# Where three weights are asked for at the start of a graph kernel, and one product of the constant fewer

## The chip, the core and the metric

The kernel runs on one core of a Trainium2 chip. Five engines work side by side, each through its own list of instructions, and wait for each other by semaphores: TensorE (PE; its weight loads are shown apart, as PEld), VectorE (DVE), ScalarE (ACT), GpSimd (POOL) and SyncE (SP). SyncE and ScalarE ask for DMA transfers, each on a queue of its own. The metric is the device time of one execution in microseconds (us); less is better.

## The reference

Sixty-four graphs of 128 nodes with 256 features go through two layers, each with a residual sum and a normalisation over the features:

```python
# layer 0: x, adj -> ReLU of the sum of three hops
Xw = X @ Wv + bv
sj = Xw @ aw[:d, 0]; si = Xw @ aw[d:, 0]
e = leaky_relu(sj[:, None, :] + si[:, :, None] + ab[0], negative_slope=0.2)
alpha = A * exp(e)
transition = alpha / (sum(alpha, axis=-1, keepdims=True) + 1e-12)
for k in range(3):
    H = H + Xk @ Wk[k] + bk[k]
    Xk = transition @ Xk
x = layernorm(x + relu(H))
# layer 1
x = layernorm(x + (adj @ x) @ w)
```

## The kernel before, in words

The graphs are worked on in 32 pairs. Each engine has one hand-written list: a start, a loop `step(k)` over the pairs, and an end. The lists are staggered; in step k of TensorE the products of W2 for pair k + 5, of W1 (and W0) for pair k + 1, the attention sums of pairs k and k + 1 and the second layer of pairs k - 1 and k - 2 are in flight.

A float32 product is made of three products of halves: ScalarE rounds a tile to its `_hi` part, GpSimd or VectorE subtracts to get the `_lo` part, and TensorE multiplies hi with hi, hi with lo, and lo with hi (line 1073). The first pair's products with W2 and W1 are taken from the full float32 tiles (`first_product`, line 1101), so that they need no split.

The start, which the change touches:

- SyncE asks for xt(0) (line 314), the transposed Wv (`WvT_sb`, line 356) and W1 (line 352), waits for xt(0), and asks for W0 (line 352) and xt(1). It waits for W2, asks for adjs(0), waits for W1, asks for xt(2) and xt(3), waits for xt(1), and asks for adjs(1), w, adjs(2) and nodes(0). Then `step(-5)` begins; from its fourth xt on, SyncE also waits for TensorE (`v1_done`) and GpSimd (`xt_lo_ready`).
- ScalarE asks for W2 (`WY_sb`, line 404), the small vectors (`vectors_sb`, 3 KB, line 405), bk (line 406) and ab (line 407). Then it loads its table and rounds: `xt_hi(0)`, `wx_hi(0)` (needs W0), `v2_hi(0)` (needs the first products of W2), `xt_hi(1)`, `first_scores()`, `xt_hi(2)`, `leaky_of(0)`, `exponentials(0)`, and so on.
- TensorE multiplies a constant by itself nine times (`keep_warm`, line 1236; 128x128 by 128x512 in bf16, with no use for the result). Then come `first_hop2(0)` (xt(0) and W2, first graph), `score_weights()` (Wv transposed times the attention vectors, line 1269; needs `WvT_sb` and `vectors_sb`), `first_hop2(1)`, `first_hop1(0)` (xt(0) and W1, needs W1 and VectorE's copy of the score weights), `score_shift()`, `first_hop1(1)`, `sum_of_biases()`, `spread_scores(0)` (needs ScalarE's first scores), `hop0(0)` and `hop2_and_scores(1)` (12 matmuls each), and `propagate_v2(0)`, the first to need alpha.
- VectorE copies the score weights beside W1 and W2 and splits W2. GpSimd sums the bias vectors (needs `vectors_sb`) and then makes `xt_lo(0)`.

W0, W1, W2, Wv, w and each xt and nodes are 256 KB; each adjs is 128 KB.

Of the kernel before, what the change touches and what calls it, by code (L numbers as in the profile page):

```python
# [10 lines left out]
P = 128  # L11
PER = 2
DMA = 16
# [5 lines left out]
def resnorm_graph_kernel(nc, xt, adjs, nodes, WvT, vectors, ab, Wk, bk, w, si_rows, out):  # L19
# [6 lines left out]
    with ExitStack() as ctx:  # L26
        def sb(name, shape, dt=F32):
            return ctx.enter_context(nc.sbuf_tensor(name, shape, dt))

        def ps(name, shape):  # L30
            return ctx.enter_context(nc.psum_tensor(name, shape, F32))

        def sem(name):
            return ctx.enter_context(nc.semaphore(name))
# [11 lines left out]
        WvT_sb = sb("WvT_sb", [P, C, D])  # L46
# [68 lines left out]
        ps_v = ps("ps_v", [P, PER, 512])  # L115
# [11 lines left out]
        xt_loaded = [sem(f"xt_loaded{s}") for s in range(4)]  # L127
# [3 lines left out]
        WvT_loaded = sem("WvT_loaded")  # L131
# [115 lines left out]
        def there(k):  # L247
            return 0 <= k < PAIRS
# [57 lines left out]
        @block.sync  # L306
        def _(sp):
            def load_xt(k):
                if k == 4:

                    sp.wait_ge(v1_done, 1)
                if k >= 4:
                    sp.wait_ge(xt_lo_ready, k - 3)
                sp.dma_start(xt_sb[k % 4][:], xt[k]).then_inc(xt_loaded[k % 4], DMA)

            def load_adjs(k):
                if k >= 5:

                    sp.wait_ge(agg_done, k - 4)
                sp.dma_start(adjs_sb[k % 5][:].rearrange("p b i -> p (b i)"),  # L320
                             adjs[k]).then_inc(adjs_loaded[k % 5], DMA)

            def load_nodes(k):
                if k >= 2:
                    sp.wait_ge(res1_ready, k - 1)
                sp.dma_start(nodes_sb[k % 2][:].rearrange("p b d -> p (b d)"),
                             nodes[k]).then_inc(nodes_loaded[k % 2], DMA)

            def store(k):
                if k < LAST - 4:  # L330
                    sp.wait_ge(out_ready, k + 1)
                else:
                    sp.wait_ge(late_out_ready, k - (LAST - 4) + 1)
                sp.dma_start(out[k],
                             out_sb[k % 3][:].rearrange("p b d -> p (b d)")).then_inc(stored[k % 3], DMA)

            def store_si(k):
                sp.wait_ge(scores_ready, k + 1)
                sp.dma_start(si_rows[k], scores[k % 3][:, 1]).then_inc(si_stored, DMA)  # L339

            def load_spread(k):

                sp.wait_ge(si_stored, DMA * (k - BY_PE + 1))
                if k >= 3:
                    sp.wait_ge(leaky_ready, k - 2)
                sp.dma_start(spread[k % 3][:].rearrange("p j b -> p (j b)"),
                             si_rows[k].rearrange("j b -> (j b)").partition_broadcast(P)
                             ).then_inc(spread_loaded[k % 3], DMA)

            def load_Wk(n):  # L350
                to = (W0_sb, W1_sb)[n]
                sp.dma_start(to[:, :, 0:D], Wk[n].rearrange("(c p) n -> p c n", p=P)).then_inc(Wk_loaded[n], DMA)


            load_xt(0)
            sp.dma_start(WvT_sb[:], WvT.rearrange("(c p) n -> p c n", p=P)).then_inc(WvT_loaded, DMA)
            load_Wk(1)
            sp.wait_ge(xt_loaded[0], DMA)
            load_Wk(0)
            load_xt(1)  # L360
            sp.wait_ge(Wk_loaded[2], DMA)
            load_adjs(0)
            sp.wait_ge(Wk_loaded[1], DMA)
            load_xt(2)
            load_xt(3)
            sp.wait_ge(xt_loaded[1], DMA)
            load_adjs(1)
            sp.dma_start(w_sb[:], w.rearrange("(c p) n -> p c n", p=P)).then_inc(w_loaded, DMA)
            load_adjs(2)
            load_nodes(0)  # L370

            def step(k):
                if there(k + 3) and k + 3 >= BY_PE:
                    load_spread(k + 3)
                if there(k + 4) and k + 4 >= BY_PE:
                    store_si(k + 4)
                if k == -3:
                    load_adjs(3)
                    load_nodes(1)
                if there(k + 1) and k > 0:  # L380
                    load_nodes(k + 1)
                if there(k + 3) and k > 0:
                    load_adjs(k + 3)
                if there(k + 9) and k >= -5:
                    load_xt(k + 9)
                if there(k - 3):
                    store(k - 3)

            for k in range(-5, LAST + 2):
                step(k)  # L390

            sp.wait_ge(late_half_out_ready, 1)
            sp.dma_start(out[LAST - 1, :, 0:D], out_sb[(LAST - 1) % 3][:, 0]).then_inc(last_stored, DMA)
            for b in range(PER):
                sp.wait_ge(last_out_ready, b + 1)
                sp.dma_start(out[LAST, :, b * D:(b + 1) * D], last_out_sb[:, b]).then_inc(last_stored, DMA)
            for slot in range(3):
                sp.wait_ge(stored[slot], DMA * len(range(slot, LAST - 1, 3)))

            sp.wait_ge(last_stored, 2 * PER * DMA)  # L400

        @block.scalar
        def _(act):
            act.dma_start(WY_sb[:, :, 0:D], Wk[2].rearrange("(c p) n -> p c n", p=P)).then_inc(Wk_loaded[2], DMA)
            act.dma_start(vectors_sb[:].rearrange("p c n -> p (c n)"), vectors).then_inc(vectors_loaded, DMA)
            act.dma_start(bk_sb[:], bk).then_inc(bk_loaded, DMA)
            act.dma_start(ab_col[:], ab.partition_broadcast(P)).then_inc(ab_loaded, DMA)

# [660 lines left out]
        def _(pe):  # L1069
# [35 lines left out]
            def first_hop2(b):  # L1105
                pe.wait_ge(xt_loaded[0], DMA)
                pe.wait_ge(Wk_loaded[2], DMA)
                last = first_product(ps_y[:, b, 0:D], WY_sb[:, :, 0:D], b)
                if b == PER - 1:
                    last.then_inc(y_done, 1)  # L1110
# [122 lines left out]
            def keep_warm(to, times):  # L1233

                for n in range(times):
                    pe.matmul(to, some[:, 0:P], some, start=True, stop=True, skip_group_check=True)  # L1236
# [77 lines left out]
                    aggregate(k - 1)  # L1314
                hop2_and_scores(k + 5, [1] if k == 1 else range(PER))

            keep_warm(ps_v[:, 0], 9)
            first_hop2(0)
            score_weights()
            first_hop2(1)  # L1320
# [68 lines left out]
```

## Time and profile before

| | before |
|---|---|
| median of 3 runs | 275.74 us |
| lowest and highest | 275.46 and 275.97 us |
| span of the profiled execution, first to last instruction | 273.8 us |
| busy: TensorE products / weight loads | 98% / 90% |
| busy: VectorE / ScalarE / GpSimd | 80% / 69% / 71% |

Busy shares are averages over the whole span. "Idle before, releaser" in a row tells how long an engine stood idle and what ended it; where a wait is for several things, the one named is the last that the profile shows, and it need not be the one that held. Products of TensorE are pipelined and their ends are modelled, so the distance from start to start is the better measure. The time of a DMA to landing counts from the start of its issue.

### The profile page before, as it was taken

What the parts mean: (1) busy time and instruction counts of PE and PEld (TensorE: products, weight loads), DVE (VectorE), ACT (ScalarE), POOL (GpSimd) and SP (SyncE); (2) the same over time, 40 slices, a digit from 0 to 9 for tenths busy, and PEclk for the clock granted to TensorE, in tenths of its full rate; (3) what the DMA queues carried; (4) which work ended last, traced back from release to release, by engine and by line L of the source; (5) the groups of instructions that cost most, each with busy time, mean ns of one, the idle gap of its engine ahead of it and who ended that gap; (6) DMA issues with size and microseconds to landing.
All of it is one profiled execution on the core that took longest, in us unless ns stands there. A gap on an engine that the chain in (4) does not pass through costs nothing.

```text
span 273.8 us, 6042 instructions
## 1 busy us (share of the span) xinstructions
PE 267.3 (98%) x1899; PEld 247.7 (90%) x1899; DVE 218.1 (80%) x615; ACT 187.9 (69%) x428; POOL 194.6 (71%) x419
## 2 busy tenths in 40 slices
PE   8999998999999999999999999999999999999993
PEld 4899988999999999999999999999999999999992
DVE  0777668888898888889888888988888898788895
ACT  2788666776667777666777766677776667765653
POOL 2576537878777787877777787777778777557564
PEclk9999999999999999999999999999999999999998
DMA  7848256458593388555873456843884348822204
GB/s 224 292 141 94 44 185 97 94 150 154 149 149 123 91 123 141 162 143 153 94 117 122 145 157 141 144 110 108 120 159 98 116 115 111 118 66 77 95 25 153
DMA packets 28758, 34.91 MB, mean 127 GB/s; under 512 B 7091, under 2 KB 16694, under 8 KB 28726
## 3 DMA queue, kind: packets, MB, share of 16 engines
q1 hardware_dynamic: 28016, 34.12, 56.4%
q10 hardware_dynamic: 710, 0.40, 0.5%
q8 instruction: 15, 0.25, 0.4%
q14 instruction: 17, 0.14, 0.2%
HBM read 26.09 MB, written 8.42 MB: 126 GB/s over the span
## 4 chain that ended last, share of the span: by engine, by line
PE 86%; DMA 5%; DVE 3%; ACT 2%; issue 1%; SPq 1%; POOL 1%; POOLq 0%; DVEq 0%; ACTq 0%
PE ps_v L1073 27%; PE ps_y L1073 14%; PE ps_out L1073 14%; PE ps_h L1073 10%; PE ps_agg L1246 9%; DMA si_rows_dram<-scores 3%; PE ps_v L1183 2%; PE ps_v L1187 2%; PE ps_v L1185 2%; DMA nodes<-nodes_dram 2%; PE ps_v L1236 1%; PE ps_y L1101 1%; SPq L339 1%; PE ps_v L1101 1%; DVE stats L777 1%
## 5 line engine op out<-in xcount | busy, mean ns | idle before, releaser
L1073 PE MATMUL ps_v<-WX_hi,XT_hi 128*128 128x512 f32 (+1 forms) x128 | 47.7, 373 | 0.0
L1073 PE MATMUL ps_v<-WX_lo,XT_hi 128*128 128x512 f32 (+1 forms) x128 | 47.4, 371 | 0.0
L1073 PE MATMUL ps_v<-WX_hi,XT_lo 128*128 128x512 f32 (+1 forms) x128 | 47.4, 370 | 0.0
L986 POOL TENSOR_TENSOR alpha<-exps,adjs 128x256 f32<-128x256 f32 x31 | 23.1, 746 | 31.3 <-ACT exps L462 26.0
L974 POOL TENSOR_TENSOR XT_lo<-xt,XT_hi 128x512 fp32r<-128x512 f32 x32 | 41.3, 1291 | 4.8 <-DVE WX_lo L891 2.7
L990 POOL TENSOR_TENSOR alpha_lo<-alpha,alpha_hi 128x256 fp32r<-128x256 f32 x31 | 22.9, 737 | 18.4 <-ACT alpha_hi L471 18.4
L494 ACT ACTIVATE y<-res,offset,rstd 128x256 f32<-128x256 f32 x62 | 33.6, 591 | 1.1 <-POOL offset L945 1.1
L1073 PE MATMUL ps_y<-WY_hi,XT_hi 128*128 128x258 f32 x112 | 34.1, 305 | 0.0
L1246 PEld LDWEIGHTS ps_agg<-adjs,y 128*128 128x128 f32 x248 | 32.0, 191 | 2.2
L1246 PE MATMUL ps_agg<-adjs,y 128*128 128x128 f32 x248 | 32.6, 274 | 0.0
L487 ACT ACTIVATE V_hi<-ps_v 128x512 fp32r<-128x512 f32 x32 | 19.1, 596 | 19.5 <-PE ps_v L1073 19.3
L1073 PE MATMUL ps_out<-w_hi,agg_hi 128*128 128x256 f32 x112 | 31.6, 282 | 0.0
L1073 PE MATMUL ps_y<-WY_hi,XT_lo 128*128 128x258 f32 x112 | 31.6, 282 | 0.0
L1073 PE MATMUL ps_y<-WY_lo,XT_hi 128*128 128x258 f32 x112 | 31.5, 282 | 0.0
L1073 PE MATMUL ps_out<-w_hi,agg_lo 128*128 128x256 f32 x112 | 31.3, 280 | 0.0
L1073 PE MATMUL ps_out<-w_lo,agg_hi 128*128 128x256 f32 x112 | 31.3, 279 | 0.0
L968 POOL TENSOR_SCALAR out_sb<-res,rstd,offset 128x256 f32<-128x256 f32 x54 | 29.6, 559 | 0.1
L479 ACT ACTIVATE ps_v<-ps_v,inv_rowsum 128x256 f32<-128x256 f32 x62 | 25.2, 444 | 5.5 <-DVE inv_rowsum L677 3.1
L1073 PEld LDWEIGHTS ps_v<-WX_hi,XT_lo 128*128 128x128 f32 x128 | 24.0, 188 | 4.6
L500 ACT ACTIVATE agg_hi<-ps_agg 128x512 fp32r<-128x512 f32 x31 | 18.5, 598 | 13.2 <-PE ps_agg L1246 13.2
L1073 PEld LDWEIGHTS ps_v<-WX_hi,XT_hi 128*128 128x128 f32 x128 | 24.1, 188 | 3.8 <-ACT ps_v L479 0.3
L1073 PEld LDWEIGHTS ps_v<-WX_lo,XT_hi 128*128 128x128 f32 x128 | 24.1, 188 | 3.4
(168 smaller groups left out, 831.5 us busy)
## 6 DMA issues: line engine op xcount, KB each, us to landing
xt<-xt_dram SPq DMA_DIRECT2D x32, 256.0 KB, 5.6
nodes<-nodes_dram SPq DMA_DIRECT2D x32, 256.0 KB, 5.6
out_dram<-out_sb SPq DMA_DIRECT2D x30, 256.0 KB, 5.3
adjs<-adjs_dram SPq DMA_DIRECT2D x32, 128.0 KB, 5.6
spread<-si_rows_dram SPq DMA_DIRECT2D x29, 128.0 KB, 4.9
W_sb<-Wk_dram SPq DMA_DIRECT2D x2, 256.0 KB, 3.8
si_rows_dram<-scores SPq DMA_DIRECT2D x29, 1.0 KB, 3.7
WY_sb<-Wk_dram ACTq DMA_DIRECT2D x1, 256.0 KB, 4.0
```

The costliest lines, as they stand in the source:

```text
L479: act.activation(ps_v[:, b, 0:D], ps_v[:, b, 0:D], ACT.Copy, scale=inv_rowsum[k % 2][:, b:b + 1]).then_inc(v_scaled, 1)
L487: act.activation(V1_hi[:], ps_v[:, :, 0:D], ACT.Copy).then_inc(v1_hi_ready, 1)
L494: last = act.activation(y[k % 3][:, b], res1[:, b], ACT.Identity, bias=offset1[:, b:b + 1], scale=rstd1[:, b:b + 1])
L500: act.activation(agg_hi[k % 2][:], agg(k), ACT.Copy).then_inc(agg_hi_ready, 1)
L968: last = pool.tensor_scalar(out_sb[k % 3][:, b], res2[k % 2][:, b], rstd2[k % 3][:, b:b + 1], offset2[k % 3][:, b:b + 1], ALU.mult, ALU.add)
L974: pool.tensor_tensor(XT_lo[k % 7][:].rearrange("p c b i -> p (c b i)"), xt_sb[k % 4][:], XT_hi[k % 7][:].rearrange("p c b i -> p (c b i)") ...
L986: pool.tensor_tensor(alpha[:], exps[:], adjs_sb[k % 5][:], ALU.mult).then_inc(alpha_ready, 1)
L990: pool.tensor_tensor(alpha_lo[k % 2][:], alpha[:], alpha_hi[k % 2][:].bitcast(F32), ALU.subtract).then_inc(alpha_lo_ready, 1)
L1073: last = pe.matmul(to, a, b, start=start and n == 0, stop=stop and n == 2, skip_group_check=True)
L1101: last = pe.matmul(to, X[:, c, b], weights[:, c], start=c == 0, stop=c == C - 1, skip_group_check=True)
L1183: pe.matmul(ps_v[:, b, 0:D + 2], alpha_hi[k % 2][:, b], V2_hi[k % 4][:, b], start=True, stop=False, skip_group_check=True)
L1246: last = pe.matmul(agg(k)[:, c, b], y[k % 3][:, b, c * P:(c + 1) * P], adjs_sb[k % 5][:, b], start=True, stop=True, skip_group_check=True)
```

## The change

Wv is asked for by ScalarE, after W2 and the small vectors, instead of by SyncE. SyncE asks for W1 after its wait for xt(0), and no longer ahead of it. TensorE makes eight products of the constant instead of nine. The amount of data and all later instructions are the same.

```diff
             load_xt(0)
-            sp.dma_start(WvT_sb[:], WvT.rearrange("(c p) n -> p c n", p=P)).then_inc(WvT_loaded, DMA)
+            sp.wait_ge(xt_loaded[0], DMA)
             load_Wk(1)
-            sp.wait_ge(xt_loaded[0], DMA)
             load_Wk(0)
             load_xt(1)
             sp.wait_ge(Wk_loaded[2], DMA)
@@
             act.dma_start(WY_sb[:, :, 0:D], Wk[2].rearrange("(c p) n -> p c n", p=P)).then_inc(Wk_loaded[2], DMA)
             act.dma_start(vectors_sb[:].rearrange("p c n -> p (c n)"), vectors).then_inc(vectors_loaded, DMA)
+            act.dma_start(WvT_sb[:], WvT.rearrange("(c p) n -> p c n", p=P)).then_inc(WvT_loaded, DMA)
             act.dma_start(bk_sb[:], bk).then_inc(bk_loaded, DMA)
             act.dma_start(ab_col[:], ab.partition_broadcast(P)).then_inc(ab_loaded, DMA)
@@
-            keep_warm(ps_v[:, 0], 9)
+            keep_warm(ps_v[:, 0], 8)
```

## Rows read from the trace of the kernel before

**Rows 1.** Busy us (and count) by engine, granted clock, DMA share, by stretch.

```profile
core 0: us, PE busy (x) PEld busy (x) DVE busy (x) ACT busy (x) POOL busy (x), PEclk, DMA share, GB/s
40.00:42.00 2.00, 0.88 (x8) 0.67 (x7) 1.93 (x7) 1.04 (x4) 1.84 (x7) 1.00 0.60 207
...
45.00:85.00 40.00, 40.00 (x283) 37.22 (x282) 33.38 (x96) 28.76 (x67) 31.31 (x66) 1.00 0.67 133
```

**Rows 2.** Waits of the weight loads, whole span: total us, times, longest us.

```profile
PEld ps_h L1073 <- DVE V_lo L709: 1.5, 2, 1.3
```

**Rows 3.** The tile nodes, the one transfer issued between 30 and 32 us.

```profile
DMA to landing us min/median/max: 7.2/7.2/7.2
```

**Rows 4.** Timeline of TensorE's products: start us, us (first start to last end).

```profile
0.76 4.00 PE L1236 MATMUL ps_v<-const-bfloat16-1.0 128*128 128x512 bf16 x9 [0.76 <-PEq L1380]
...
4.12 0.63 PE L1236 MATMUL ps_v<-const-bfloat16-1.0 128*128 128x512 bf16 x1
...
4.86 1.42 PE L1101 MATMUL ps_y<-WY_sb,xt 128*128 128x256 f32 x4
...
5.68 0.60 PE L1101 MATMUL ps_y<-WY_sb,xt 128*128 128x256 f32 x2
```

**Rows 5.** Timeline of SyncE's queue, the issues of the first 4.9 us.

```profile
0.72 0.38 SPq L314 DMA_DIRECT2D xt<-xt_dram  x1
1.16 0.42 SPq L356 DMA_DIRECT2D WvT_sb<-WvT_dram  x1
1.63 2.77 SPq L352 DMA_DIRECT2D W_sb<-Wk_dram  x2
```

**Rows 6.** The tile xt: xt(0) and xt(1) (one row), then xt(2), issued at 6.30.

```profile
DMA to landing us min/median/max: 3.3/3.3/3.3
...
DMA to landing us min/median/max: 3.4/3.4/3.4
```

**Rows 7.** Timeline of ScalarE and its queue, first 4.9 us.

```profile
0.73 0.47 ACTq L404 DMA_DIRECT2D WY_sb<-Wk_dram  x1
...
1.75 0.56 ACTq L406 DMA_DIRECT2D bk_sb<-bk_dram  x1
...
2.72 1.28 ACT L412 ACT_TABLE_LOAD   x1 [2.72 <-issue]
```

**Rows 8.** DMA issues: KB each, median us from issue to landing.

```profile
nodes<-nodes_dram SPq DMA_DIRECT2D x32, 256.0 KB, 5.6
...
WY_sb<-Wk_dram ACTq DMA_DIRECT2D x1, 256.0 KB, 4.0
WvT_sb<-WvT_dram SPq DMA_DIRECT2D x1, 256.0 KB, 4.3
...
vectors_sb<-vectors_dram ACTq DMA_DIRECT2D x1, 3.0 KB, 4.4
```

**Rows 9.** DMA queues from 0 to 3.5 us: packets, MB, share of 16 engines.

```profile
q10 hardware_dynamic: 116, 0.12, 9.5%
```

**Rows 10.** The same from 3.5 to 4.2 us.

```profile
q10 hardware_dynamic: 153, 0.14, 57.9%
q1 hardware_dynamic: 123, 0.13, 50.5%
```

**Rows 11.** The same from 4.2 to 5 us.

```profile
q10 hardware_dynamic: 146, 0.01, 11.7%
```

**Rows 12.** Timeline of all engines from 5.9 to 10.3 us.

```profile
5.90 1.08 PEld L1269 LDWEIGHTS ps_out<-vectors_sb,WvT_sb 128*128 128x128 f32 x8
...
7.08 0.63 ACT L417 ACTIVATE WX_hi<-W_sb 128x512 fp32r<-128x512 f32 x1 [2.41 <-DMA W_sb<-Wk_dram]
...
7.66 0.84 PEld L1101 LDWEIGHTS ps_v<-W_sb,xt 128*128 128x128 f32 x4
...
8.07 0.60 ACT L442 ACTIVATE V_hi<-ps_y 128x512 fp32r<-128x512 f32 x1 [0.36 <-PE ps_y L1101]
...
10.04 0.26 ACT L428 ACTIVATE scores<-ps_v,shift 128x4 f32<-128x4 f32 x1 [0.85 <-PE ps_v L1101]
10.20 0.62 ACT L412 ACTIVATE XT_hi<-xt 128x512 fp32r<-128x512 f32 x1
```

## The prediction

> **What bounds the kernel now.** I read the table by stage first. From 45 us on TensorE has work in all of its time, 40.00 us of 40.00; before that it has gaps, the largest between 40 and 42 us [rows 1]. So nothing that the change touches can make the long middle shorter. It touches only the loading at the start, and a gain there counts as far as it moves everything behind it forward. The waits of the weight loads name one long wait after the start, 1.3 us for a V_lo of VectorE [rows 2]. That V_lo stands in VectorE's order behind the residual of pair 2, which needs nodes(2), and nodes(2) took 7.2 us to land [rows 3]. I return to it as a rival.
>
> Then the start itself. Nine products of the constant run from 0.76, the last from 4.12: (4.12 - 0.76) / 8 = 0.42 us for 512 columns, which is 1.2 GHz. The last one's columns are through at about 4.54, and the first product of X starts at 4.86, not at 4.54 [rows 4]. The view names xt as the releaser, but xt(0) was asked for at 0.72 and took 3.3 us, so it was there at 4.02 [rows 5, 6]. W2 was asked for at 0.73 and took 4.0 us: 4.73 [rows 7, 8]. So W2 ends TensorE's wait, and the last 0.2 to 0.3 us before 4.86 are a wait for a DMA that one product of the constant fewer does not shorten. The clock is still low there: the first two half products of X take 5.68 - 4.86 = 0.82 us, while the two from 5.68 on lie 0.60 - 0.38 = 0.22 us apart. The clock rose to 2.4 GHz at about 5.5 [rows 4]. (The granted-clock column shows 1.00 for this stretch too, so I read the level from the spacing.)
>
> **Part 1: what stands beside W2 in the DMA engines.** Up to 3.5 us the ScalarE queue (q10) moved 0.12 MB, from there to 4.2 another 0.14 MB; together that is W2's 0.26 MB, so its data was through at about 4.2. In the second stretch SyncE's queue (q1) moved 0.13 MB, nearly all of it Wv [rows 9, 10]. In the new kernel q1 has nothing behind xt(0) until W1 is asked for at about 4.0. W2's last 0.14 MB then have the engines alone: at the rate of that stretch, 0.27 MB in 0.70 us or 386 GB/s, 0.36 us instead of 0.70. W2 lands some 0.33 us earlier, at 4.40. The bounds: 0 (the bandwidth was not what held it) and 0.71 (W2 as early as xt(0), 4.02; W0 needed 3.05 us from issue, 4.03, to its use at 7.08, with others beside it [rows 5, 12]). I take 0.33, because both queues show their bytes in just that stretch.
>
> **Part 2: one product of the constant fewer.** It ends at 4.12 instead of 4.54. With W2 at 4.40, plus the 0.13 us from landing to start (4.86 - 4.73), the first product of X starts at 4.53. With nine products it would have started at about 4.54 too. So this edit by itself is worth nothing, to 0.1 us: it only takes away a bound that would just begin to hold. If W2 lands at once with xt(0), it is worth up to 4.54 - 4.15 = 0.39 us of start, half of that in time.
>
> What does the earlier start give? Until about 5.5 the clock is low. Work begun 0.33 us earlier runs those 0.33 us at half speed, so from 5.5 on TensorE is 0.33 / 2 = 0.16 us ahead. The ends are 0 and 0.71 / 2 = 0.35 us.
>
> **Part 3: Wv on ScalarE's queue.** Before, it landed at 1.16 + 4.3 = 5.46 [rows 5, 8], and the weights of its products were loaded from 5.90 on, behind the products of X and without a wait [rows 12]. In the new kernel they could start at 5.74. Wv is asked for after the small vectors, at 1.75, when bk was before [rows 7]. In the engines it follows W2 (through at 3.87) and the vectors. Its own 0.26 MB at 386 GB/s take 0.67 us, and from data to landing W2 took 4.73 - 4.2 = 0.53. That makes 3.87 + 0.67 + 0.53 = 5.07 if the vectors' 128 rows cost nothing. They took most of the 0.8 us from 4.2 to 5.0 (146 packets, 0.01 MB) beside a full q1 [rows 11]: 5.87 at that price. I take the middle, 5.5: no wait. A wait at the upper end is 5.87 - 5.74 = 0.13 us. The other upper bound is the vectors' own 4.4 us from issue [rows 8]: 1.75 + 4.4 = 6.15, and with Wv's data behind that 6.82. It is the slower rival.
>
> ScalarE's own instructions shift by one issue, some 0.5 us: bk and ab are asked for later, the table load runs 3.2 to 4.5 instead of 2.72 to 4.00 [rows 7], and XT_hi(0) behind it ends by 5.2. The next activation starts at 7.08 after 2.41 us of idling [rows 12], and GpSimd takes XT_hi(0) up only behind its work on the vectors, which land at 1.2 + 4.4 = 5.6 [rows 7, 8]. So this is hidden, by 0.4 us of cover at the least.
>
> **Part 4: W1 behind xt(0) on SyncE's queue.** SyncE stands on xt(0) until 4.03 (1.63 + 2.77, less the 0.37 of W0's own issue). Before, W0 was asked for then and was in use 3.05 us later, at 7.08 [rows 5, 12]. Now W1 takes that place: 7.08 at the latest, where it had been there at 6.30, when SyncE went on to xt(2). TensorE wants it after the second half of W2's products, at 7.66 - 0.16 = 7.50 [rows 12]: 0.42 us of cover. W0 is one issue later (0.42 us, Wv's): about 7.5. It holds ScalarE's WX_hi, which started at 7.08, until 7.5; it then ends at 8.13, and V_hi follows, which started at 8.07 after 0.36 us of idling [rows 12]. That cover is all but used up; what is over, some 0.1 us, goes into the 0.85 us that ScalarE idles before the first scores. xt(1) lands at 4.9 + 3.3 = 8.2 [rows 6], before that V_hi is done. Behind the wait for W1 stand xt(2) and xt(3): asked for at 7.08 instead of 6.30, xt(2) lands at 7.08 + 3.4 = 10.5 [rows 6] where its XT_hi started at 10.20 [rows 12], and the first attention scores stand behind that on ScalarE. This could cost 0.3 us of ScalarE's time, and 0.46 against the shifted order; but what waits on it, the first alpha, is wanted by TensorE only behind 12 matmuls with W0 and 12 with W2. I take 0, with 0.3 as the upper bound; W1 landing sooner than W0 did, with less ahead of it in q1, speaks for 0.
>
> **Sum.** Span 273.8 - 0.16 = 273.6 us. The median of the runs before lies 1.94 us above the span of the profiled one (275.74 against 273.8), and that stays: 275.74 - 0.16 = 275.6 us.
>
> **The rivals.**
> *Nothing moves (0.20).* W2 was late for its own latency. TensorE then starts at 4.86 again, with 0.74 us of empty array ahead instead of 0.32. For it: xt(0) had the engines with half of W2 only and still took 3.3 us. Against it: the bytes of Wv that went in between [rows 10]. Time: 275.7. The Trainium skill points this way: DMA: Bandwidth & Descriptors, "Issuing engines are not separate DMA queues", says that DMAs from any engine share the same 16 DMA engines and interleave, so that another issuer saves only issue time. By that rule alone moving Wv would bring nothing. But the change also keeps W1 back, and between 3.5 and 4.2 us the two queues did share the engines [rows 10]; so I give the rule's result the smaller chance.
>
> *Wv comes late: slower (0.13).* Wv stands behind three rows of work on ScalarE's queue. It costs from the point where it lands after 5.64 (its products at 5.74). At 6.15 the net is 0.51 - 0.16 = +0.35: 276.1; at 6.82 it is 1.18 - 0.16 = +1.02: 276.8. All that follows waits: u, both W1 products, the scores. Over 0.55 us of loss needs a landing after 6.35.
>
> *A gap in the constant's products delays the clock: slower (0.05).* Low clock lasted from 0.76 to 5.5. Each microsecond more of it costs half a microsecond. Against it: at 40 to 42 us TensorE idled 1.1 us and the clock stayed up [rows 1], though that is a clock already up. One more microsecond: 275.74 + 0.5 - 0.16 = 276.1.
>
> *The late stall moves: faster (0.12).* nodes(2) took 7.2 us where the median of all 32 is 5.6 [rows 3, 8]. Had it taken 5.6, VectorE would go on 1.6 us earlier, and the 1.3 us in which TensorE waits [rows 2] would be gone. A shifted order of DMAs could do this: 275.6 - 1.3 = 274.3. Against it: the runs before agree to 0.5 us, and nothing in the change reaches that transfer but 0.16 us of shift.
>
> *Forecast (0.50):* 275.6, of itself 275.2 to 275.9.
>
> **Range and chances.** The measurement can tell 0.2% from no change, 0.55 us. The forecast and "nothing moves" lie inside; even the upper end of the start's gain, 0.35 us, does. Faster by more: the late stall, and a little for a gain of 0.35 with the scatter of the runs: 0.16. Slower by more: the far half of the late Wv, the clock, and a missed cover in part 4: 0.14. Same: 0.70. The range 274.9 to 276.2 leaves out the moved stall and the far end of the late Wv.
>
> **What would show it.** Right: the first product of X at 4.5 to 4.6, W2 landing in 3.6 to 3.8 us; the products of Wv directly behind, without a wait; W0 in ScalarE's WX_hi at about 7.5; the first scores on ScalarE at about 9.9 instead of 10.04; everything from 14 us on 0.1 to 0.2 us earlier. Wrong: the first product of X again at 4.86; a wait of the weight loads of Wv's products or of the W1 products on a DMA; low-clock spacing after 5.6; another length of the wait at 41 us, which would outweigh all else.

## The result, and the profile after

| | before | changed |
|---|---|---|
| median | 275.27 us | 276.4 us |
| lowest and highest, 22 executions each | 274.3 and 276.4 us | 274.79 and 280.91 us |
| ratio, with its 95% interval | | 1.0044 (1.0026 to 1.0061) |
| span of the profiled execution | 273.8 us | 273.1 us |

The change is slower, by over 0.2%. The median is 276.4, above the upper end of the range (276.2). Seven of the 22 executions took over 277.5 us, and none of before did. The ratios, here and below, leave out executions more than 1.5% above the fastest of their kernel, here the two longest of these seven (279.61 and 280.91 us), so they understate the loss.

The profiled execution of the changed kernel was one of its quick ones, 274.87 us. It shows what the moved transfers do, and not what makes the median. Its page, busy time and share of the span:

```profile
span 273.1 us, 6040 instructions
...
PE 266.9 (98%) x1898; PEld 247.6 (91%) x1898; DVE 217.9 (80%) x615; ACT 188.0 (69%) x428; POOL 194.0 (71%) x419
```

The start in the view in order of time (start, length, engine, line, operation, idle before and releaser), to be read against [rows 4 to 7, 12]. First TensorE and its weight loads:

```profile
0.76 3.57 PE L1236 MATMUL ps_v<-const-bfloat16-1.0 128*128 128x512 bf16 x8 [0.76 <-PEq L1380]
4.77 1.50 PE L1101 MATMUL ps_y<-WY_sb,xt 128*128 128x256 f32 x4 [0.45 <-DMA WY_sb<-Wk_dram]
...
5.89 1.08 PEld L1269 LDWEIGHTS ps_out<-vectors_sb,WvT_sb 128*128 128x128 f32 x8
6.11 0.95 PE L1269 MATMUL ps_out<-vectors_sb,WvT_sb 128*128 128x2 f32 x8
6.92 1.11 PE L1101 MATMUL ps_y<-WY_sb,xt 128*128 128x256 f32 x4
...
8.88 1.12 PE L1101 MATMUL ps_v<-W_sb,xt 128*128 128x258 f32 x4
...
10.55 0.43 PE L1165 MATMUL ps_out<-identity,scores 128*128 128x128 f32 x2
```

Then the queues of ScalarE and SyncE, and ScalarE's work:

```profile
1.74 0.46 ACTq L405 DMA_DIRECT2D WvT_sb<-WvT_dram  x1
...
3.96 0.90 SPq L352 DMA_DIRECT2D W_sb<-Wk_dram  x2
4.90 0.47 SPq L314 DMA_DIRECT2D xt<-xt_dram  x1
...
6.71 0.80 SPq L314 DMA_DIRECT2D xt<-xt_dram  x2
...
7.42 0.63 ACT L417 ACTIVATE WX_hi<-W_sb 128x512 fp32r<-128x512 f32 x1 [2.27 <-DMA W_sb<-Wk_dram]
...
8.98 0.63 ACT L412 ACTIVATE XT_hi<-xt 128x512 fp32r<-128x512 f32 x1 [0.31 <-DMA xt<-xt_dram]
...
10.03 0.26 ACT L428 ACTIVATE scores<-ps_v,shift 128x4 f32<-128x4 f32 x1 [0.43 <-PE ps_v L1101]
...
10.49 0.63 ACT L412 ACTIVATE XT_hi<-xt 128x512 fp32r<-128x512 f32 x1 [0.20 <-DMA xt<-xt_dram]
```

The first product of X starts at 4.77, where it had started at 4.86 [rows 4]. The products of Wv follow at 6.11, without a wait for a DMA, as before, and the last product of W1 (8.88) and the step behind the scores (10.55) stand where they stood, to 0.01 us. ScalarE's WX_hi begins 0.34 us later than it did [rows 12] and its XT_hi(2) 0.29 us later, while the first scores stand where they stood. ScalarE now waits 0.31 us for xt(1) ahead of XT_hi(1), whose start in the trace of before was 8.57.

The DMA issues, with the median time to landing in the last column, against [rows 8]; and ScalarE's queue (packets, MB, share of 16 engines) up to 3.5 us, against [rows 9]:

```profile
WY_sb<-Wk_dram ACTq DMA_DIRECT2D x1, 256.0 KB, 3.9
...
WvT_sb<-WvT_dram ACTq DMA_DIRECT2D x1, 256.0 KB, 3.6
```

```profile
q10 hardware_dynamic: 246, 0.19, 16.0%
```

ScalarE's queue had 0.19 MB through by 3.5 us, against 0.12 [rows 9]. Yet W2 landed at 0.72 + 3.9 = 4.62 (4.64, if the 0.13 us from landing to start are as before), and not 0.33 us earlier. Neither difference is steady: two more traces of this same kernel (e7 and e14 below) have 0.14 and 0.03 MB through by 3.5 us, and their first product of X starts at 4.82 and 5.09. Around 41 us, against [rows 1, 2]:

```profile
PEld ps_h L1073 <- DVE V_lo L709: 0.6, 2, 0.5
```

The wait for V_lo is 0.5 us at the longest, where it had been 1.3. That, 0.8 us, is as much as the two spans differ by (0.7 us); the experiments below show that it scatters from trace to trace.

### The profile page after: what moved, and what is told of

It reads as the page before. It is cut to its first block, busy times and chain, and to the rows that moved or that the text cites. A ratio compares the mean times of both kernels' runs of the same rounds, so it can differ in the third digit from the quotient of the medians.

```text
span 273.1 us, 6040 instructions
## 1 busy us (share of the span) xinstructions
PE 266.9 (98%) x1898; PEld 247.6 (91%) x1898; DVE 217.9 (80%) x615; ACT 188.0 (69%) x428; POOL 194.0 (71%) x419
## 4 chain that ended last, share of the span: by engine, by line
PE 86%; DMA 6%; DVE 2%; SPq 1%; POOL 1%; ACT 1%; issue 1%; POOLq 0%; DVEq 0%; ACTq 0%
PE ps_v L1073 27%; PE ps_y L1073 14%; PE ps_out L1073 14%; PE ps_h L1073 10%; PE ps_agg L1246 9%; DMA si_rows_dram<-scores 3%; PE ps_v L1183 3%; PE ps_v L1187 3%; PE ps_v L1185 3%; DMA nodes<-nodes_dram 2%; DMA WY_sb<-Wk_dram 1%; PE ps_y L1101 1%; SPq L339 1%; PE ps_v L1101 1%; DVE stats L777 1%
```

## The experiments

Each ran in five rounds beside the kernel before. The edits are against the kernel before unless another is named. The expectations call the theories by letters. C: with the array empty ahead of the first product of X, the clock rises late. V: Wv comes late. X: xt(2), asked for behind the wait for W1, comes late. P: xt(1) comes late, and GpSimd's subtraction then runs beside VectorE's first alpha. L: the wait at 41 us makes the difference, through nodes(2) and adjs(4). D: the two DMA edits by themselves cost 0.55 us. "Long" is an execution above 277.5 us.

### The edits one by one

```diff
-            keep_warm(ps_v[:, 0], 9)
+            keep_warm(ps_v[:, 0], 8)
```

> Only edit: eight products of the constant instead of nine; every DMA as before. Theory X (a late xt(2) costs the time; it comes of W1 being held back): 1.000 within 0.002, the first product of X at 4.8 to 4.9 as before. Theory C (the emptier TensorE ahead of the first product of X makes the clock rise late in some executions, half a us per us): 1.003 or more, with single runs several us long. Theory V (Wv lands late in some executions): 1.000.

Measured: 276.18 us (274.48 to 279.31) against 275.32, ratio 1.0011 (0.998 to 1.0042), 5 long of 12. Its profiled execution is a long one, span 277.5:

```profile
0.76 3.57 PE L1236 MATMUL ps_v<-const-bfloat16-1.0 128*128 128x512 bf16 x8 [0.76 <-PEq L1380]
4.96 2.05 PE L1101 MATMUL ps_y<-WY_sb,xt 128*128 128x256 f32 x4 [0.63 <-DMA WY_sb<-Wk_dram]
6.80 1.71 PE L1269 MATMUL ps_out<-vectors_sb,WvT_sb 128*128 128x2 f32 x8
8.36 2.05 PE L1101 MATMUL ps_y<-WY_sb,xt 128*128 128x256 f32 x4
10.21 1.93 PE L1101 MATMUL ps_v<-W_sb,xt 128*128 128x258 f32 x4
```

The four products of W2 take 2.05 us each time, where the same four take 1.11 us at the high clock (6.92 in the changed kernel), and the eight of Wv 1.71 us, not 0.95. This is 1.2 GHz, until about 13.5 us. One product of the constant fewer, alone, brings the long executions.

```diff
-            sp.dma_start(WvT_sb[:], WvT.rearrange("(c p) n -> p c n", p=P)).then_inc(WvT_loaded, DMA)
@@
+            act.dma_start(WvT_sb[:], WvT.rearrange("(c p) n -> p c n", p=P)).then_inc(WvT_loaded, DMA)
```

> Only edit: Wv asked for on ScalarE's queue behind W2 and the small vectors; W1 stays ahead of SyncE's wait for xt(0), nine products of the constant. Theory X: 1.000 within 0.002 (W1 and xt(2) as early as before or earlier). Theory C: 1.000. Theory V: 1.003 or more, and the products of Wv waiting on a DMA after 5.9.

Measured: 276.46 (274.6 to 277.84), ratio 1.0027 (0.9997 to 1.0058).

```profile
5.03 1.33 PE L1101 MATMUL ps_y<-WY_sb,xt 128*128 128x256 f32 x4 [0.27 <-DMA WY_sb<-Wk_dram]
6.63 1.02 PE L1269 MATMUL ps_out<-vectors_sb,WvT_sb 128*128 128x2 f32 x8 [0.27 <-DMA WvT_sb<-WvT_dram]
```

Here the products of Wv do wait for Wv, 0.27 us, and start 0.51 us later than before (6.12); part of that is the later start of X (5.03). Wv took 4.8 us to land, against 3.5 to 4.1 in the nine traces that also hold W1 back. So the rival was real as long as W1 was asked for early; with W1 held back, it is not. Three executions lie at 277.54 to 277.84, with a lower recorded clock (0.989 to 0.990); none was profiled, and what they are stays open.

```diff
-            load_Wk(1)
             sp.wait_ge(xt_loaded[0], DMA)
+            load_Wk(1)
```

> Only edit: W1 asked for after SyncE's wait for xt(0); Wv stays on SyncE, nine products of the constant. Theory X: 1.003 to 1.005, xt(2) asked for some 0.4 us later than 6.30, XT_hi(2) at about 10.5 instead of 10.20 and propagate_v2(0) at about 13.97 instead of 13.81. Theories C and V: 1.000.

Measured: 275.76 (275.14 to 276.19), ratio 1.001 (0.9985 to 1.0035), none long. No difference that can be told.

Both edits of the transfers, with nine products (e2's and e3's together):

> Both DMA edits together, nine products of the constant. Theory X: 1.004, as the whole change. Theory C: 1.000, because the ninth product fills the wait for W2 as before. Theory V: 1.004.

Measured: 275.8 (275.1 to 276.55), ratio 1.0021 (1.0003 to 1.0039), none long.

```profile
9.78 0.63 ACT L412 ACTIVATE XT_hi<-xt 128x512 fp32r<-128x512 f32 x1 [0.93 <-DMA xt<-xt_dram]
...
10.48 2.54 POOL L974 TENSOR_TENSOR XT_lo<-xt,XT_hi 128x512 fp32r<-128x512 f32 x2 [3.42 <-ACT XT_hi L412]
...
12.35 0.95 DVE L635 TENSOR_TENSOR alpha<-exps,adjs 128x256 f32<-128x256 f32 x1 [0.86 <-ACT exps L462]
```

```profile
14.49 0.36 PE L1183 MATMUL ps_v<-V_hi,alpha_hi 128*128 128x258 f32 x1 [0.57 <-DVE alpha_lo L639]
```

xt(1) took 4.7 us to land, so ScalarE waited 0.93 us for it. GpSimd's two subtractions ran until 10.48 + 2.54 = 13.02, beside VectorE's first alpha. That took 0.95 us, and TensorE's first product with alpha started at 14.49. The same two lines in the trace of before:

```profile
12.20 0.42 DVE L635 TENSOR_TENSOR alpha<-exps,adjs 128x256 f32<-128x256 f32 x1 [0.51 <-ACT exps L462]
...
13.81 0.36 PE L1183 MATMUL ps_v<-V_hi,alpha_hi 128*128 128x258 f32 x1
```

### How many products of the constant

```diff
-            keep_warm(ps_v[:, 0], 9)
+            keep_warm(ps_v[:, 0], 7)
```

> Only edit against the kernel before: seven products of the constant. TensorE is then empty from 3.7 to the first product of X at 4.9. Theory C (emptier TensorE ahead of the first product of X makes the clock rise late in some executions): more such executions than with eight (five of 12 there above 277.5 us): half or more above 277.5, ratio 1.006 to 1.012. Rival (the count of products is of no account, the long runs with eight were of the chip): none above 277.5, ratio 1.000.

Measured: 278.52 (275.54 to 279.22), ratio 1.0113 (1.0073 to 1.0152), 5 long of 6.

```profile
4.87 2.05 PE L1101 MATMUL ps_y<-WY_sb,xt 128*128 128x256 f32 x4 [0.97 <-DMA WY_sb<-Wk_dram]
```

The same with 10 in place of 7:

> Only edit against the kernel before: ten products of the constant, the last one's columns through at about 4.97. Theory C: no execution above 277 us, ratio 0.998 to 1.001 (the first product of X up to 0.15 us later at the low clock, no late rise). Rival: 1.000 with the same scatter as before.

Measured: 275.61 (274.35 to 276.68), ratio 1.0003 (0.998 to 1.0025), none long. With 7, 8, 9 and 10 products ahead of X in the kernel before, 5 of 6, 5 of 12, 2 of 165 (the runs of before of all sessions) and 0 of 12 executions are long.

The changed kernel once more, with no edit:

> The changed kernel once more, word for word, for more executions of it and another profile. Theory C: a quarter to a half of the executions above 277.5 us, where the two kernels with W1 held back and nine products had none of 24; ratio 1.004 to 1.008. If the profile falls on a long one, the low-clock spacing of 0.42 us lasts far beyond 6 us.

Measured: 277.04 (274.94 to 279.69), ratio 1.0037 (1.0008 to 1.0067), 6 long of 12.

The changed kernel with 10 products:

```diff
-            keep_warm(ps_v[:, 0], 8)
+            keep_warm(ps_v[:, 0], 10)
```

> The change, but with ten products of the constant instead of eight. Theory C: no execution above 277.5 us (the change itself had 13 of 34), and what is left is the cost of the DMA edits, 1.001 to 1.003. Rival (the long executions are made by the DMA edits together with fewer products): still some above 277.5.

Measured: 275.65 (274.42 to 276.47) against 275.39, ratio 1.0005 (0.9991 to 1.0019), none long. Two products more in the changed kernel take away its long executions and nearly all of its loss. What the tenth product costs at the start cannot be read from single traces. The last product of W1, at 8.88 before and in the change, stands 0.34 and 0.62 us later in e6's and e9's:

```profile
9.22 1.12 PE L1101 MATMUL ps_v<-W_sb,xt 128*128 128x258 f32 x4
```

```profile
9.50 1.12 PE L1101 MATMUL ps_v<-W_sb,xt 128*128 128x258 f32 x4
```

But in e13's trace, also with ten, it stands at 8.62, and in six with nine (e3, e4, e8, e11, e12, e16) at 8.39 to 9.16. What moves it is mostly the rise of the clock, which the traces' own clock records put at 6.13 us in e6, 6.70 in e9 and 4.78 in e13. The ratios of e6 and e9, 1.0003 and 1.0005, show no cost either.

Eight products, and the ninth behind the first two of X's groups (the kernel before; the amount of work is the same):

```diff
-            keep_warm(ps_v[:, 0], 9)
+            keep_warm(ps_v[:, 0], 8)
             first_hop2(0)
+            keep_warm(ps_v[:, 0], 1)
```

> The kernel before, but the ninth product of the constant stands behind the first two products of X and W2 instead of ahead of them: the amount of work in the first 6 us is the same, the emptiness ahead of the first product of X is that of eight. Theory C (it is the emptiness ahead of that product that counts): a third or more of the executions above 277.5 us, ratio 1.002 to 1.008. Rival (the total of products counts): none above 277.5, ratio 1.000 to 1.001.

Measured: 275.93 (274.91 to 280.12), ratio 1.0018 (0.9992 to 1.0045), 5 long of 12. So the place counts, ahead of the first product of X, and not the number. No run separates the two things that the missing product changes there: the unbroken work is shorter by one product, and the gap behind it is longer.

```profile
4.94 1.10 PE L1101 MATMUL ps_y<-WY_sb,xt 128*128 128x256 f32 x4 [0.61 <-DMA WY_sb<-Wk_dram]
5.88 0.38 PE L1236 MATMUL ps_v<-const-bfloat16-1.0 128*128 128x512 bf16 x1
```

This trace is of a quick execution: it waits as long ahead of X as e1's (4.94 and 4.96), and the clock was high at once (its record has the rise at 4.44, within the gap). So the length of the wait alone does not decide a single execution. What does stays open.

The changed kernel a third time, with no edit:

> The changed kernel word for word, a third time. Theory C: a quarter to a half of the executions above 277.5 us; a profile of one of them shows the products of X at the low-clock spacing (0.42 us from start to start instead of 0.22) to beyond 9 us and everything behind 3 to 4 us later. Rival (with the change the long executions have another cause than the one traced with eight products alone): a profiled long execution with its clock risen at about 5.5.

Measured: 277.22 (274.73 to 279.85) against 275.32, ratio 1.0055 (1.0021 to 1.0088), 6 long of 12; the mean of all twelve is 277.24. This time the profiled execution is a long one, 278.45 us with a span of 276.6:

```profile
0.76 3.57 PE L1236 MATMUL ps_v<-const-bfloat16-1.0 128*128 128x512 bf16 x8 [0.76 <-PEq L1380]
5.09 2.05 PE L1101 MATMUL ps_y<-WY_sb,xt 128*128 128x256 f32 x4 [0.76 <-DMA WY_sb<-Wk_dram]
6.93 1.71 PE L1269 MATMUL ps_out<-vectors_sb,WvT_sb 128*128 128x2 f32 x8
8.50 2.05 PE L1101 MATMUL ps_y<-WY_sb,xt 128*128 128x256 f32 x4
10.35 1.93 PE L1101 MATMUL ps_v<-W_sb,xt 128*128 128x258 f32 x4
12.06 0.42 PE L1276 MATMUL ps_agg<-const-float32-1.0,bv_aw_sum 128*128 128x1 f32 x2
12.35 1.12 PE L1101 MATMUL ps_v<-W_sb,xt 128*128 128x258 f32 x4
...
14.03 0.43 PE L1165 MATMUL ps_out<-identity,scores 128*128 128x128 f32 x2
```

Against the quick execution of the same kernel, above: everything up to 12.06 runs at half speed, and from 12.35 on the lengths are those of the quick one. The step behind the scores starts at 14.03, where the quick one has it at 10.55: 3.48 us, and the spans differ by 276.6 - 273.1 = 3.5. What is lost at the start is never given back, since TensorE has no idle time from 45 us on to give it from [rows 1]. The traces' clock records agree: the rise is at 12.36 us here and at 5.58 in the quick execution, 6.8 us more at half speed, 3.4 us.

### What the moved transfers cost

e4, with xt(2) no longer held back by W1:

```diff
             load_adjs(0)
-            sp.wait_ge(Wk_loaded[1], DMA)
             load_xt(2)
```

> Both DMA edits, nine products, and SyncE no longer waits for W1 before it asks for xt(2) and xt(3) (they go into other buffers, so nothing else changes). Theory X (the DMA edits cost because xt(2), adjs(1) and what follows come late): xt(2) asked for at about 6.1 instead of 6.97, XT_hi(2) without a wait at 10.3, the weight loads of propagate_v2(0) without their 0.7 us wait; ratio 1.000, against 1.002 with the wait. Rival (the loss of the DMA edits is elsewhere, or scatter): 1.002 again.

Measured: 276.09 (274.9 to 278.19), ratio 1.0035 (1.0014 to 1.0056).

```profile
9.62 0.63 ACT L411 ACTIVATE XT_hi<-xt 128x512 fp32r<-128x512 f32 x1 [0.69 <-DMA xt<-xt_dram]
```

xt(2) asked for earlier took nothing off the loss: theory X fell. The line shows xt(1), not xt(2), to be late. One execution is long (278.19, recorded clock 0.993; the two of before have 0.992 and 0.993).

The same trace shows an empty array that did no harm:

```profile
0.76 3.50 PE L1235 MATMUL ps_v<-const-bfloat16-1.0 128*128 128x512 bf16 x9 [0.76 <-PEq L1379]
5.19 1.10 PE L1100 MATMUL ps_y<-WY_sb,xt 128*128 128x256 f32 x4 [0.94 <-DMA WY_sb<-Wk_dram]
```

The nine products took 3.50 us and not 4.00, since the clock rose during them (at 3.61 by its record). TensorE then idled 0.94 us, longer than in e14's long execution (0.76), and the clock stayed up. In all four long executions that were profiled the gap lies ahead of the rise; a gap behind it, as here, did nothing.

e4, with xt(1) asked for ahead of W1 and W0:

```diff
             sp.wait_ge(xt_loaded[0], DMA)
+            load_xt(1)
             load_Wk(1)
             load_Wk(0)
-            load_xt(1)
```

> Both DMA edits, nine products, and SyncE asks for xt(1) ahead of W1 and W0 after its wait for xt(0). Theory P (the DMA edits cost because xt(1) lands up to 2 us later, GpSimd's XT_lo(1) and XT_lo(2) then run beside VectorE's first alpha, which takes 0.95 us instead of 0.42, and propagate_v2(0) starts at 14.49 instead of 13.81): XT_hi(1) without a wait for a DMA, alpha back at 0.42, propagate_v2(0) at 13.7 to 13.9, ratio 1.000 unless W1, now later, holds TensorE before its products at 7.7. Rival (the loss is elsewhere): 1.002 again.

Measured: 276.25 (275.19 to 276.61) against 275.39, ratio 1.0026 (1.0008 to 1.0044). XT_hi(1) still started at 9.51, now behind a WX_hi that waited for W0 until 8.50 (7.42 in the change), and XT_hi(2), at 10.97, waited 0.62 us. The wait went from one transfer to the next; this order on the queue does not cure it.

### The wait at 41 us

nodes(2) and adjs(4) are asked for in step 0 instead of step 1:

```diff
-                if there(k + 1) and k > 0:
+                if k == 0:
+                    load_nodes(2)
+                    load_adjs(4)
+                if there(k + 1) and k > 1:
                     load_nodes(k + 1)
-                if there(k + 3) and k > 0:
+                if there(k + 3) and k > 1:
                     load_adjs(k + 3)
```

> The kernel before, but SyncE asks for nodes(2) and adjs(4) in its step 0, behind the store of scores(4), instead of in step 1, behind the issue that takes 2.2 us at 28.3. Theory L (TensorE's 1.3 us wait at 41 us comes of nodes(2) and adjs(4) landing at 38, and its size, 0.3 to 1.7 us from trace to trace, is most of the scatter of the undisturbed runs): the residual of pair 2 and alpha(4) without a wait for a DMA, TensorE's wait at 41 us under 0.3, ratio 0.995 to 0.997. Rival (something else is late at 41 us): ratio 0.999 to 1.001.

Measured: 274.12 (273.72 to 274.71) against 275.32, ratio 0.996 (0.9942 to 0.9978).

```profile
PEld ps_h L1076 <- DVE V_lo L712: 0.2, 1, 0.2
```

```profile
23.53 0.43 SPq L326 DMA_DIRECT2D nodes<-nodes_dram  x1
...
28.36 2.60 SPq L339 DMA_DIRECT2D si_rows_dram<-scores  x1
```

SyncE's write of the scores at 28.3 us took 2.60 us to issue (2.27 in the trace of before, 2.18 in that of the change; the ordinary issue beside it 0.43). In the kernel before, nodes(2) stood behind it. Asked for ahead of it, it lands in time, the wait at 41 us is 0.2 us, and the twelve executions lie within 1.0 us, where those of before spread over 2.6 (273.63 to 276.27). By trace, that wait was 1.3 us before, 0.5 in the change, and 0.3 to 1.7 in the eleven traces of e1 to e11: it differs between executions of kernels that have the same work there.

The changed kernel with 10 products and this edit:

> Both DMA edits of the change, ten products of the constant, and nodes(2) and adjs(4) asked for in step 0. Theories C and L together: no execution above 277.5 us, ratio 0.996 to 0.999, some 0.001 to 0.002 above the same without the DMA edits. If the DMA edits' loss is only a shift of when the wait at 41 us is paid: the same ratio as without them.

Measured: 274.67 (274.27 to 274.96), ratio 0.9981 (0.9962 to 1.0001), none long. Against e12, of the same session, that is 0.55 us more.

e12 with 8 products:

> nodes(2) and adjs(4) early as before, Wv and W1 where the kernel before has them, eight products of the constant instead of nine. Theory C: two heaps of executions, one at 274.0 to 274.8 us as with nine products, the other (a quarter to a half of them) 3.2 to 4.2 us above. Rival (one product fewer costs nothing): one heap at 274.0 to 274.8.

Measured: 274.03 against 274.02, ratio 1.0021 (0.9989 to 1.0052). With the scatter gone, the two kinds of execution stand apart: nine at 273.75 to 274.38, and three at 277.75, 277.80 and 278.09. Nothing lies in the 3.37 us between. The profiled one is long:

```profile
4.86 2.04 PE L1104 MATMUL ps_y<-WY_sb,xt 128*128 128x256 f32 x4 [0.53 <-DMA WY_sb<-Wk_dram]
...
12.12 1.50 PE L1104 MATMUL ps_v<-W_sb,xt 128*128 128x258 f32 x4
```

e12 with both edits of the transfers and nine products:

> nodes(2) and adjs(4) early, both DMA edits, nine products of the constant. Theory D (the 0.55 us that the same kernel with ten products lies above the one without the DMA edits are the DMA edits): median 274.5 to 274.8. Rival (they are the tenth product): 274.1 to 274.3.

Measured: 274.43 (273.9 to 274.69) against 274.02, ratio 1.0009 (0.9999 to 1.0019), none long. So the transfers cost 0.4 us by the medians (the ratio's interval reaches from 0 to 0.5). The median lies between what theory D and its rival said, so how the 0.55 us are shared between the transfers and the tenth product stays open.

In this last session the kernel before took 274.02 us in the middle, without any edit (273.61 to 274.93), and in e16's trace the issue at 28 us was an ordinary one (the next, at 34.39, took 1.61 us); in e15's none was slow. So e12 beats both kernels by 0.4% in a session where the slow issue comes. That it gains nothing where the issue does not come is likely but not shown: neither e12 nor a trace of before was taken in the last session, only e15, whose nine quick executions lie where before's do.

## Why the prediction was wrong

**What bounds the kernel: right.** A loss at the start goes through to the end in full, 3.48 us of 3.5.

**Part 1, W2's landing: the 0.33 us did not come.** In the change's trace the landing moved from 4.73 to some 4.64, 0.09 us, and that is within the scatter: W2 took 3.8 to 4.3 us to land in the nine traces with both edits of the transfers (4.04 in the mean), and 4.0 to 4.3 in the seven with the transfers of before (4.09). Whether bandwidth beside W2 held it at all stays open; its share is far below 0.33 us. "Nothing moves" was right here. The Trainium skill points this way (DMA: Bandwidth & Descriptors, "Issuing engines are not separate DMA queues"): by that rule another issuer saves only issue time. The traces agree, with 4.04 against 4.09 us.

**Part 2, one product fewer: the step that decided.** It said that this edit is worth nothing, since it only takes away a bound that would just begin to hold. With W2 hardly earlier, it took away cover instead. The eighth product's columns are through at 0.76 + 8 × 0.42 = 4.12, and the array stood empty until 4.77 to 5.09 in the traces of the kernels with eight, 0.65 to 0.97 us, where before it was 0.32 (with nine products at the low clock, 0.60 at the most, in e12). In those kernels with the change's order (22 + 12 + 12 executions) 19 of 46 were long; in e1, e10 and e15 13 of 36. Of the kernels with nine or ten ahead of X, e3, e4, e6, e9, e11, e12, e13 and e16 had none in 95; before had 2 in 165, e8 1 in 12 and e2 3 in 12. These six lie at 277.54 to 278.19 with a recorded mean clock of 0.989 to 0.993, and none was profiled. They are probably of another kind, for the four long executions that were profiled have 0.997 to 1.000, as the quick ones have. Two of the long ones with eight products have 0.992 as well (280.91 in the change, 277.96 in e10), so the counts 19 and 13 may each be one too high. In the three long traces above, and in e5's, the clock stays at 1.2 GHz until 12 to 13.5 us.

**The clock rival: the right name, priced at a seventh and given 0.05.** It took one microsecond more of low clock, 0.5 us. Measured were 6.8 us more and 3.5 us. The 19 long executions of the change have a mean of 278.81 us, its 27 others 275.78, and before, in the same three sessions, 275.33: of the 1.70 us of loss in the mean the long ones make 1.25, and 0.45 are in the others too. The argument against it was that the clock stayed up over 1.1 us of idling at 41 us [rows 1]. That row shows a clock already up. It says nothing of one not yet up, as the prediction noted and then discounted.

**Part 3, Wv: right.** No wait; it landed at 1.74 + 3.6 = 5.34, against 5.5. e2 shows what it is without W1 held back: a wait, and the products 0.51 us later than before.

**Part 4, W1, W0 and xt: three of four right, one missed.** WX_hi at 7.42 (7.5 was said), XT_hi(2) at 10.49 (10.5), the first scores not moved to 9.9 but also not later (10.03). Missed was xt(1): it was given the 3.3 us of [rows 6], but now stands behind W1, W0 and Wv and took 4.1 us in the change and 4.7 in e4. That moves GpSimd's XT_lo(1) and (2) beside VectorE's first alpha, the one overlap that the prediction never looked at:

```profile
11.20 1.29 POOL L974 TENSOR_TENSOR XT_lo<-xt,XT_hi 128x512 fp32r<-128x512 f32 x1 [0.25 <-ACT XT_hi L412]
```

```profile
12.19 0.59 DVE L635 TENSOR_TENSOR alpha<-exps,adjs 128x256 f32<-128x256 f32 x1 [0.51 <-ACT exps L462]
...
13.97 0.36 PE L1183 MATMUL ps_v<-V_hi,alpha_hi 128*128 128x258 f32 x1
```

In the change it is mild, 0.59 us for alpha against 0.42, and TensorE 0.16 us later at its first product with alpha. In e4, e8 and e11 it was 0.95, 0.87 and 0.65 us, and TensorE came there at 14.34 to 14.49. Alpha's end is set by GpSimd: in the eight traces with both transfer edits and an early rise (the change, e4, e7, e8, e9, e11, e13, e16) it lies 0.27 to 0.29 us behind the end of GpSimd's second subtraction, though alpha itself takes from 0.53 to 0.95 us. Before, that subtraction had ended at 12.19 and alpha started at 12.20. In e11 and e16 there is a second part: alpha starts 0.4 and 0.3 us later, because the exponentials stand on ScalarE behind XT_hi(2), which waited 0.62 and 1.07 us for xt(2). The Trainium skill (SBUF — State Buffer, "🔬 SBUF: two separate sides") says that a VectorE instruction with two inputs from SBUF and a GpSimd one that reads SBUF exclude each other at a shared port. The traces agree, with 0.95 against 0.42 us. Over all, the transfers cost 0.1 to 1.0 us by the ratios of e4, e8, e9, e11 and e16 (1.0005 to 1.0035). Their sign is against the 0.16 us of gain in the sum. (The 0.0005 is e9's, which has the tenth product too.) What in them varies with the execution (xt(1)'s landing, 4.1 or 4.7 us for the same edits) stays open.

**The late stall: right on what it rests, wrong on how steady it is.** The prediction took the agreement of three runs to 0.5 us as evidence that the stall is fixed. It scatters by over a microsecond, and the single span of the changed kernel, shorter than before's by 0.7 us, owes that to it. Whoever had read the two spans alone would have called the change faster.

**The sum.** Said was 275.6 (274.9 to 276.2): -0.16 from the start. Measured is 276.4. The start gave no gain that can be told from scatter, the transfers cost 0.1 to 1.0 us (0.45 in the quick executions of the change), and the late clock costs 3.5 us in 4 of 10 executions, 1.25 us in the mean. The term that was put at nothing, one product of the constant fewer, is the largest of the three.

## What to carry to other kernels

Work with no use that keeps TensorE busy up to its first real product should not be shortened on a landing that is only forecast: no run shows a price of one product more (e6, ratio 1.0003), and one fewer costs 3.5 us in four of ten executions. A one-sided price like that is to be weighed with its worst case, and a row that shows the clock staying up says nothing about whether it will come up. Where a change can split executions in two kinds, read the whole list of times before any profile, for a profile is of one execution.

## What was not expected of the hardware

- In one and the same kernel, the changed one, TensorE's clock rose at 5.6 and 5.7 us in two traces and at 12.4 in the third. Over all 18 traces its clock records put the rise at 3.61 to 6.70 us in fourteen and at 12.18 to 13.46 in four, never between; in e15 no time lies in the 3.37 us between the two kinds. Two executions with equal waits ahead of X (e1: 4.96, e10: 4.94) went different ways.
- The view's granted-clock column shows 1.00 for the slow stretch too. It has to be read from the spacing of equal products, or from the first rise on record.
- One issue of a DMA on SyncE, at 28 to 29 us (31 to 32 in the long traces), took 1.95 to 2.72 us in 15 of the 18 traces. In e13's, e15's and e16's the one at 28 us (e15: 26 and 31) took 0.43, and in e16's the next took 1.61. Why, no run shows.
- When ScalarE's first transfer moves its bytes scatters in one and the same kernel: 0.19, 0.14 and 0.03 MB through by 3.5 us in the three traces of the change.
